# Router logits of the feed-forward layers computed with the router's weights held in TensorE

## The reference

```python
# f1 and f2: 8 routed experts, top 2 by sigmoid plus a bias, and a dense shared part of 1024 hidden units
# f3 and f4: 16 routed experts, top 2 by softmax
scores = jax.nn.softmax(xf @ gate_w.T, axis=-1)
topk_w, topk_idx = jax.lax.top_k(scores, K)
topk_w = topk_w / (jnp.sum(topk_w, axis=-1, keepdims=True) + 1e-20)
combine = jnp.zeros((T, E), dtype=xf.dtype).at[jnp.arange(T)[:, None], topk_idx].add(topk_w)
g = jnp.einsum('th,ehi->tei', xf, wg)
u = jnp.einsum('th,ehi->tei', xf, wu)
a = jax.nn.silu(g) * u * combine[:, :, None]
y = jnp.einsum('tei,eih->th', a, wd)
```

## Time and profile before

| what | value |
|---|---|
| runs (three) | 1933.06 / 1937.61 / 1937.88 us |
| the profiled execution's own time | 1934.87 us |
| its span | 1933.0 us, 27525 instructions |
| PE busy | 1597.6 us (83%), 9322 matmuls |
| DVE busy | 1091.6 us (56%) |
| ACT busy | 910.5 us (47%) |
| POOL busy | 710.4 us (37%) |
| f1 starts its loads | 218.5 us |
| f2 starts its loads | 421.35 us |
| f3 starts its loads | 717.16 us |
| f4 starts its loads | 1787.62 us |

### The profile page before, as it was taken

One profiled execution on the slowest core, in us unless ns is written; L12 is line 12 of the kernel. 1 busy time (PEld: TensorE's weight loads), 2 busy tenths in 40 slices (PEclk: granted clock), 3 DMA queues, 4 the chain that ended last, 5 costly groups with the idle time before them and its releaser, 6 DMA issues. The chain is left out here.

```text
span 1933.0 us, 27525 instructions
## 1 busy us (share of the span) xinstructions
PE 1597.6 (83%) x9322; PEld 1179.4 (61%) x9322; DVE 1091.6 (56%) x2136; ACT 910.5 (47%) x1926; POOL 710.4 (37%) x695
## 2 busy tenths in 40 slices
PE   6899798779876872927999999999999999998373
PEld 4444578668853432825776677667777677776262
DVE  4665354665457984446555655565555665554533
ACT  2365344234424322525555566556555565654341
POOL 3011260415145746047434443444343444420703
PEclk9899799888987995868999999999999999999586
DMA  3321334213424014430000000000000000000543
GB/s 77 51 51 43 117 99 126 80 50 109 126 67 175 1 39 143 140 107 17 15 9 12 6 12 17 12 6 12 12 6 12 12 9 12 6 6 1 164 145 101
DMA packets 80216, 106.59 MB, mean 55 GB/s; under 512 B 12337, under 2 KB 64177, under 8 KB 79697
## 3 DMA queue, kind: packets, MB, share of 16 engines
q1 hardware_dynamic: 73936, 88.04, 15.3%
q0 software_dynamic: 6144, 16.79, 2.7%
HBM read 70.64 MB, written 27.72 MB: 51 GB/s over the span
## 5 line engine op out<-in xcount | busy, mean ns | idle before, releaser
L1307 DVE TENSOR_SCALAR_CACHE_REDUCE gqa_scaled<-acc,gqa_neg_scale 128x128 bf16<-128x128 f32 (+7 forms) x256 | 208.8, 816 | 312.5 <-PE acc L1459 311.0
L1479 PE MATMUL aux<-gqa_probsT,gqa_v 128*128 128x512 f32 (+3 forms) x768 | 272.1, 491 | 11.2 <-DVE gqa_turned_k L1263 7.0
L1200 ACT ACTIVATE gqa_probsT<-aux 128x512 f32<-128x512 f32 (+3 forms) x384 | 174.5, 490 | 188.3 <-PE aux L1470 188.3
L1190 ACT ACTIVATE gqa_probs<-acc,gqa_bias,gqa_q_scale 128x128 f32<-128x128 f32 (+7 forms) x256 | 213.5, 834 | 46.2 <-DVE gqa_scaled L1307 39.9
L1084 POOL TENSOR_TENSOR gqa_q_high<-gqa_straight,gqa_turned_q 128x512 fp32r<-128x512 f32 x64 | 87.7, 1371 | 327.6 <-DVE gqa_turned_q L1263 327.6
L1479 PEld LDWEIGHTS aux<-gqa_probsT,gqa_v 128*128 128x128 f32 x768 | 138.3, 190 | 102.9 <-issue 62.1
L1470 PE MATMUL aux<-ident,gqa_probs 128*128 128x128 f32 x1152 | 169.0, 274 | 0.3 <-ACT gqa_probsT L1200 0.3
L1458 PE MATMUL acc<-gqa_k_high,gqa_q_high 128*128 128x512 f32 (+3 forms) x384 | 156.4, 407 | 7.4 <-DVE gqa_k_low L1291 5.7
L1458 PE MATMUL acc<-gqa_k_high,gqa_q_low 128*128 128x512 f32 (+3 forms) x384 | 133.3, 347 | 0.0
L1458 PE MATMUL acc<-gqa_k_low,gqa_q_high 128*128 128x512 f32 (+3 forms) x384 | 132.9, 346 | 0.0
L1470 PEld LDWEIGHTS aux<-ident,gqa_probs 128*128 128x128 f32 x1152 | 124.6, 141 | 0.6 <-issue 0.4
(11 more groups left out here) (412 smaller groups left out, 4324.6 us busy)
## 6 DMA issues: line engine op xcount, KB each, us to landing
f_w<-in_f_up SPq DMA_DIRECT2D x64, 256.0 KB, 2.8
f_xs<-tokens_by_slot SPq DMA_DIRECT2D x108, 128.0 KB, 2.2
outputs_by_slot<-f_y_tile SPq DMA_DIRECT2D x108, 128.0 KB, 1.7
f_w<-in_f_down SPq DMA_DIRECT2D x64, 128.0 KB, 3.2
mat_qk<-mat_high SPq DMA_DIRECT2D x64, 64.0 KB, 2.3
scan_b_all<-scan_rows SPq DMA_DIRECT2D x1, 4096.0 KB, 22.2
gqa_w_q<-in_g_wq SPq DMA_DIRECT2D x32, 128.0 KB, 2.0
gqa_wo<-in_g_wo SPq DMA_DIRECT2D x32, 128.0 KB, 2.0
```

Source lines behind the costliest of these rows:

```text
L1190: act.activation(probs_of(t, 0, t + 1), scores(t), ACT.Exp, bias=bias[:, n % 16:n % 16 + 1], scale=q_scale[:, h // 2 % 2, h % 2 * NT + t:h ...
L1200: act.activation(turned_tile(t, a, b), aux[:, chunk(n, c) % 2, 0:(b - a) * P].rearrange("p (s w) -> p s w", w=P), ACT.Copy).then_inc(chunk ...
L1307: dve.tensor_scalar(scaled[:, 0:width(t)], scores(t), neg_scale[:, h // 2 % 2, h % 2 * NT + t:h % 2 * NT + t + 1], None, ALU.mult, ALU.min ...
L1479: last = pe.matmul(weigh_bank(half)[:, first:], v[:, h // GQ % 2, s, :], moving, start=s == 0, stop=s == 4 * half + 3)
```

## The change

Three edits, all in the feed-forward layers.

1. **The router's product.** High and low part of the weights now lie side by side in one tile `w_router_parts` (16 columns in f1 and f2, 32 in f3 and f4). They are the held side, and the high and then the low part of the tokens are streamed, 256 tokens (one pair) at a time: `project(q)`, 4 matmuls for a pair, 16 in all. The result has experts on partitions, with the halves for high and low weights one below the other. ACT copies it to SBUF (`take_parts`, into `xs`, which is free then). `fold_parts(q)` makes two small matmuls for a pair, one per token tile: the copied parts are the held side and `fold` (two identities, one below the other) is streamed, which adds the two halves and puts tokens on partitions again. These are full f32 matmuls. Low x low is now part of the sum.
2. **The bias's own wait.** The bias has a semaphore of its own, which DVE waits for just before it adds the bias. ACT starts on the router's weights when these alone are there.
3. **The router's low part later.** DVE makes it, and `fold`, after the statistics of the first pair instead of ahead of them (`between`).

With them ACT's order changes: the first three weight splits stand between the norm's copies, and `split(3)` and what follows stand behind `take_parts(3)`.

```diff
-    def vector(self, dve):
+    def vector(self, dve, between=None):
...
             if q < NT // 2:
                 statistics(q)
+            if between is not None and q == 0:
+                between()
...
-        w_router_high = sb("w_router_high", [P, DC, routed], F32R)
-        w_router_low = sb("w_router_low", [P, DC, routed], F32R)
+        w_router_parts = sb("w_router_parts", [P, DC, 2 * routed], F32R)
+        w_router_high, w_router_low = w_router_parts[:, :, 0:routed], w_router_parts[:, :, routed:]
+        fold = sb("fold", [2 * routed, routed])
...
+        parts = [aux[0:2 * routed, bank, 0:2 * P] for bank in (0, 1, 3, 0)]
+        parts_sb = [xs[0:2 * routed, q, 0:2 * P] for q in range(NT // 2)]
...
-                sp.dma_start(bias[:, :], bias_dram.rearrange("(a e) -> a e", a=1).to_broadcast([P, routed])).then_inc(router_in, 16)
+                sp.dma_start(bias[:, :], bias_dram.rearrange("(a e) -> a e", a=1).to_broadcast([P, routed])).then_inc(bias_in, 16)
...
-            act.wait_ge(router_in, 32 if bias_dram is not None else 16)
-            act.activation(w_router_high[:, :, :], w_router[:, :, :], ACT.Copy).then_inc(w_router_high_ready, 1)
+            act.wait_ge(router_in, 16)
+            act.activation(w_router_high, w_router[:, :, :], ACT.Copy).then_inc(w_router_high_ready, 1)
+            def take_parts(q):
+                act.wait_ge(parts_ready, q + 1)
+                act.activation(parts_sb[q], parts[q], ACT.Copy).then_inc(parts_out, 1)
+
             split(0)
-            norm.scalar(act)
+            norm.high(act, 0)
+            split(1)
+            norm.high(act, 1)
+            split(2)
+            norm.high(act, 2)
+            take_parts(0)
+            norm.high(act, 3)
+            for q in range(1, NT // 2):
+                take_parts(q)
             if shared:
-                split(1)
-                split(2)
                 act.wait_ge(logits_ready, 1)
...
-            dve.wait_ge(w_router_high_ready, 1)
-            dve.tensor_tensor(w_router_low[:, :, :], w_router[:, :, :], w_router_high[:, :, :].bitcast(F32),
-                              ALU.subtract).then_inc(w_router_low_ready, 1)
-            norm.vector(dve)
+            def router_low():
+                dve.wait_ge(w_router_high_ready, 1)
+                dve.tensor_tensor(w_router_low, w_router[:, :, :], w_router_high.bitcast(F32),
+                                  ALU.subtract).then_inc(w_router_low_ready, 1)
+                dve.tensor_tensor(fold[:, :], core.ident[0:2 * routed, 0:routed], core.ident[0:2 * routed, routed:2 * routed],
+                                  ALU.add).then_inc(fold_ready, 1)
+
+            norm.vector(dve, router_low)
...
+                dve.wait_ge(bias_in, 16)
                 s.then(dve.tensor_tensor(select[:], probs[:], bias[:, :].unsqueeze(1).to_broadcast(wide), ALU.add))
...
-            norm.tensor(pe)
+            def project(q):
+                pe.wait_ge(norm.low_ready, q + 1)
+                if q == 3:
+                    pe.wait_ge(parts_out, 1)
+                pair = slice(2 * q * P, (2 * q + 2) * P)
+                for k in range(DC):
+                    pe.matmul(parts[q], w_router_parts[:, k, :], core.xnT_high[:, k, pair], start=k == 0, stop=False)
+                    last = pe.matmul(parts[q], w_router_parts[:, k, :], core.xnT_low[:, k, pair], start=False,
+                                     stop=k == DC - 1)
+                last.then_inc(parts_ready, 1)
+
+            def fold_parts(q):
+                pe.wait_ge(parts_out, q + 1)
+                for t in (2 * q, 2 * q + 1):
+                    last = pe.matmul(aux[:, 2, t * routed:(t + 1) * routed], parts_sb[q][:, t % 2 * P:(t % 2 + 1) * P],
+                                     fold[:, :], start=True, stop=True)
+                return last
+
+            for q in range(3):
+                norm.turn(pe, q)
             pe.wait_ge(w_router_low_ready, 1)
-            for t in range(NT):
-                pe.wait_ge(norm.low_ready, t // 2 + 1)
-                for k in range(DC):
-                    rows = slice(t * P, (t + 1) * P)
-                    for m, (a, b) in enumerate(three(core.xnT_high[:, k, rows], core.xnT_low[:, k, rows],
-                                                     w_router_high[:, k, :], w_router_low[:, k, :])):
-                        last = pe.matmul(aux[:, 2, t * routed:(t + 1) * routed], a, b, start=k + m == 0,
-                                         stop=(k, m) == (DC - 1, 2))
+            project(0)
+            norm.turn(pe, 3)
+            project(1)
+            project(2)
+            pe.wait_ge(fold_ready, 1)
+            fold_parts(0)
+            fold_parts(1)
+            project(3)
+            fold_parts(2)
+            last = fold_parts(3)
             last.then_inc(logits_ready, 1)
```

31 lines of the change are left out of this document (20 added, 11 removed).

## The result

| what | before | after |
|---|---|---|
| four runs each, median | 1936.55 us | 1909.40 us (1907.79 to 1910.37) |
| ratio | | 0.9862, 95% interval 0.9845 to 0.9879 |
| the profiled execution's own time, its span | 1934.87, 1933.0 us | 1909.48, 1907.7 us |
| f1 to the next layer's start | 149.76 us | 138.60 us |
| f2 | 148.10 | 139.55 |

The kernel became 27 us faster. I had forecast 17.65 and a range that ends at 1912, so the gain was larger than the range allowed. The starts of the layers say where it came from. f1 gained 11.16 where 6.45 was forecast, f2 8.55 (6.7), f3 with the attention behind it 3.49 (2.25), f4 3.0 (2.25). Of the other stretches, whose code is unchanged, the one ahead of f1 gained 0.84, and those ahead of f2 and f3 lost 0.26 and 1.47. Together that is 25.3, the difference of the two spans.

A forecast was written before the change was run, and what follows sets the result against it. PE, through its router, was taken to set the pace in f1 and f2, the router chain with POOL holding DVE in f3 and f4; 6.45 + 6.7 + 2.25 + 2.25 = 17.65 off the 1937.61 median gave 1920.0 us, range 1912 to 1931.

The forecast's parts named there:

- The norm's start: Ahead of the router: first statistics run while weights fly, gaining 2.65 us in f1, 2.9 in f2, 1.0 each in f3, f4.
- The fold at the low clock: In the router on PE: each small full f32 fold matmul priced at 0.43 us, as two loads of the held side.
- POOL held DVE in f3 and f4: In the choice of experts: five DVE instructions wait on POOL's low parts, leaving 2.25 us gain a layer instead of 4.8.
- The step that failed: PE's clock in f1, f2: rises 4.0 and 5.9 us after `up(0)` as before, keeping gains of 6.45 and 6.7 us.
- The gap that I expected on POOL: In f3 and f4: POOL idles between its third and fourth low part, the fourth waiting for `split(3)`; no size given.
- My picture that the mask starts when POOL ends: In f4: the choice steps through POOL's five instructions; the mask starts at 1811.9 instead of 1814.15, 2.25 us earlier; f3 likewise.
- the chain behind the mask: In f3 and f4: count, index and scatter form a plain chain that keeps its lengths, so the 2.25 us gain carries through.
- The clock by time since steady work: Rival, chance 0.10: clock answers to time since first steady work; `up(0)` runs 8.3 us low in f1, not 4.0; 1924 us.
- dear folds: Rival, chance 0.08: in the router on PE each fold costs 0.85 us; 1931 us.
- Cheap folds: Rival: folds at 0.213 us each in the router; about 1915 us; chance 0.16 shared with a free DVE.
- A free DVE: Rival: POOL does not hold DVE, so f3 and f4 gain 4.8 us each; 1915 us; chance 0.16 shared with cheap folds.
- The clock that stays down: Rival, chance 0.03: less steady work ahead keeps the low clock through all of the dense part; 45 us slower, 1982 us.

The follow-up runs named there:

- e4: The changed kernel with every fold matmul issued twice (same result); 1920.54 us, ratio 0.9929.
- e2: The kernel before with only the bias's own wait and the router's later low part, keeping the 48 narrow router matmuls; 1928.51 us, ratio 0.9962.
- e1: The changed kernel with only the router's new product; bias wait and low part put back as before; 1918.52 us, ratio 0.9913.
- e3: The kernel before with twelve 512-column bf16 matmuls of zeros between the turns and the narrow router; 1940.29 us, ratio 1.0034.
- e5: The changed kernel with ACT's splits 1 and 2 moved behind its four copies of the logit parts; 1916.49 us, ratio 0.9911.
- e6: The changed kernel with five low halves on POOL instead of eight in f3 and f4, three on DVE; 1909.12 us, ratio 0.9864.
- e8: The changed kernel with ten 512-column matmuls of zeros ahead of the first sparse tile in f3 and f4; 1910.74 us, ratio 0.9876.
- e10: The changed kernel with DVE making the experts' numbers right behind the index, ahead of its splits, in f3 and f4; 1909.59 us, ratio 0.9869.
- e15: e14 plus ten 512-column matmuls of zeros on PE between the reads of the experts' numbers and the first sparse turn; 1897.66 us, ratio 0.9806.
- e13: The changed kernel with DVE making the experts' numbers before the index, right behind the running sum, in f3 and f4; 1905.62 us, ratio 0.9844.
- e14: e13 with five low halves on POOL instead of eight in f3 and f4; 1896.16 us, ratio 0.9796.
- e7: The changed kernel with wide matmuls of zeros at each feed-forward layer's start (16 in f1 and f2, 8 in f3 and f4); 1909.30 us, ratio 0.9872.
- e11: e10 with five low halves on POOL instead of eight in f3 and f4; 1900.86 us, ratio 0.9831.

## Why the prediction was wrong

**Right.** The norm's start: the scaling came 2.82 us earlier in f1 (2.65 forecast), 3.1 in f2 (2.9), 1.16 in f3 (1.0). The last turn of f1 came 2.53 earlier (2.2). The fold at the low clock, 0.43, is e4's 0.45. POOL held DVE in f3 and f4 as expected, in five of the choice's steps. That there would be a gain beyond 0.3% was right. The start edits alone, 7.55 in my terms, measured 6.3 (e2).

**The step that failed** is the clock: "It then rises as long after `up(0)` as before, and the gain stays whole." From four stretches at 0.50 I read that PE's clock answers to wide matmuls. e1, e2 and e3 bear this out. But then I counted only the dense ones as wide and took the new projections, which stream 256 columns, to be like the old router's 8 or 16. In every layer of the changed kernel the clock rose during the router. Its parts in f1:
- From the first projection behind the last turn to `up(0)`: 4.19 us (226.64 to 230.83) instead of 5.95. Projections at 0.12 instead of 0.21 and folds at 0.25 instead of 0.43 make that.
- The dense part: no time at the low clock. I had read 4.0 us from the kernel before, where the clock in fact came up 4.3 us after `up(0)` (244.75); 46% of that is 2.0. The later 3.4 us at the low clock, which I had not seen, are gone too: 1.6.
- `up(0)` came 8.8 us after the layer's start earlier than before (13.16 instead of 21.93), where 6.45 was forecast. With 2.0 and 1.6 that makes 12.4, and the first sparse turn came 12.4 us earlier; 11.16 was left at the layer's end.

In f2 `up(0)` came 8.3 earlier (6.7), with 3.4 us of the dense part at the low clock instead of 6.0. That makes 9.5; the first sparse turn came 9.6 earlier, and 8.55 was left. Why both layers lose about 1 us behind that turn, no run explains. Together the two layers are 6.6 us over the forecast. The rule of the Trainium skill (TensorE: Matmul & The Clock Gate, Part 1), that the warm-up is a matter of busy time, I weighed and set aside. By it I had 4.5 us of this, so its result was nearer than mine. But the trace does not bear it out for narrow matmuls: the router before kept PE fully busy for 10.2 us with no rise, and in e3 PE was busy for all 2.98 us of the stretch behind which the clock fell. What the runs show is between the two: PE busy with wide matmuls.

**f3 and f4** gained 4.9 (3.49 with the attention) and 3.0 instead of 2.25 each. It is the same step: there too the end of the projections and the folds ran at the high clock (in f4 eight records in 0.99 us, 0.25 a fold). So the choice began 13.9 us behind f4's start where I had 15.7, and POOL's fourth low part at 14.0 where I had 15.3. The gap that I expected on POOL was 0.2 us in f4 and none in f3. My picture that the mask starts when POOL ends gave a fair number, 24.3 us for f4's mask against 23.2, partly by luck: in e5 the mask was done 1.7 us ahead of POOL. And the chain behind the mask was not what I took it for: in the kernel before and in the changed one the first sparse tile followed the reads of the experts' numbers, which followed the splits, and not the scatter. This did not change the term, since mask, index, splits and numbers move together in the changed kernel.

**The rivals.** The clock by time since steady work (1924) is refuted by e3, where it rose 4.4 us after the steady work began and not 14, and dear folds (1931) by e4. Cheap folds (1915) came true in size, but through the clock: a fold took 0.25 at the high clock, and 0.45 at the low one for which I had priced it. A free DVE did not come true. The clock that stays down (1982) did not, though e4 shows it in small: a little more narrow work ahead of the dense part costs several microseconds.

**What stays open.** f1's code is the same in ten profiles (both of the changed kernel, e6, e8, e10 to e15). In six of them it took 137.3 to 137.5 us and the clock stayed up in the dense part; in e13 it was down there once for 3.4 us (138.8); in e10, e14 and e15 twice (140.7 to 140.9). PE's stretches of e10:

```profile
225.25:228.25 3.00, 3.00 (x25) 1.00 0.07 25
228.75:231.50 2.75, 2.75 (x8) 0.50 0.52 142
245.75:248.75 3.00, 3.00 (x16) 0.50 0.54 194
```

The first rise comes 8.7 to 9.2 us after the layer's start in the six and in e13, and 9.35 to 9.5 in the other three. So in f1 a rise that comes late against the router's work is followed by falls. In f2 the time of the rise does not tell: at 11.6 us it was followed by a fall in e6 and by none in e8 and in the second profile of the changed kernel. The later of the falls in f1 has something ahead of it: PE idles 1.8 us in the dense part, waiting for DVE's low part of the hidden units, and in the kernel before, e1, e2, e7, e10 and e13 to e15 the clock falls 2.7 to 3.3 us after this idle time begins. But the six in which the clock stayed up have the same idle time. So what decides whether it falls, and what sets the time of the rise, these runs don't show. A part of f1's 11 us, up to 3.4, and of f2's 8.6, some 2, is not certain. With one profile of each program nothing says whether it changes from build to build or from execution to execution; four executions of the changed kernel side by side spread over 8 us.

## What to carry to other kernels

When a change replaces narrow matmuls by wide ones, price it twice, at either level of the granted clock, and let the range reach to the faster one from the first wide matmul on. And narrow the window round a rise of the clock before its time goes into a sum: mine was 0.3 us off. Before a chain is priced as "scatter, then load, then first tile", look what PE's queue does in the same time: here 31 reads at 0.65 us hid a gain of 7 us in each of two layers until they were started earlier. And a move on one engine is worth its full length only if no long run of another engine now falls on the step behind it: DVE's seven splits made one scatter issue 6.47 us long.

## What the hardware showed that I had not expected

- TensorE fell from 2.4 to 1.2 GHz while it ran matmuls of 8 columns back to back without idling, after 28 of them (e3, f1). It also fell while PE was busy with 256-column matmuls, 0.9 us behind an idle time of 1.8 us (e10, at 245.6).
- A read of a number from SBUF into a register of PE's queue is recorded with 0.30 us, but with the two instructions behind it 31 reads stand 0.65 to 0.68 us apart. From the numbers to the next matmul it is 20.1 to 20.4 us in the kernel before, the changed one and e6, where nothing else held it.
- An indirect DMA issue on POOL, 0.96 us alone, took 6.47 and 6.48 us in f3 of e10 and e11 (7.36 in f4 of e10) when DVE's run of two-input instructions of 768 columns began between the first issue and this one (0.5 us before it in e10), and 1.24 to 1.60 for the first four issues when it began ahead of the first.
- A full f32 matmul with 128 columns held and 8 or 16 streamed takes 0.25 us at the high clock, and 0.43 to 0.45 at the low one, in two records (e4).
